# Attention over eight images in four layers: double banks for row scores, one product burst for two groups, small products moved into both bank rings

## The reference

```python
h = group_norm(x) * gamma + beta
q, k, v = w_qkv @ h + b_qkv          # per head: 16 x 1024
w = softmax((q.T @ k) / sqrt(16))    # per head: 1024 x 1024
out = x + w_proj @ (w @ v) + b_proj
```

## Time and profile before

| what | value |
|---|---|
| runs | 2506.1, 2512.8, 2544.4 us, median 2512.8 |
| profiled execution | 2514.5 us, span 2512.8 us |
| mean granted clock of TensorE | 0.948 of 2.4 GHz |
| PE busy | 2274.7 us (91%) |
| DVE busy | 1809.0 us (72%) |
| ACT busy | 1721.5 us (69%) |
| POOL busy | 401.3 us (16%) |

### The profile page before, as it was taken

How to read it: one execution, slowest core, us unless ns; L and a number is a source line. 1 busy time by engine, 2 the same in 40 slices (tenths; PEclk the granted TensorE clock), 3 DMA queues, 4 the chain that set the end, 5 groups by cost and what they waited for, 6 DMA issues and landing times. The chain is left out here.

```text
span 2512.8 us, 34220 instructions
## 1 busy us (share of the span) xinstructions
PE 2274.7 (91%) x11776; PEld 1093.3 (44%) x11776; DVE 1809.0 (72%) x3172; ACT 1721.5 (69%) x3107; POOL 401.3 (16%) x631
## 2 busy tenths in 40 slices
PE   2989898989999998989898989999897999999999
PEld 1333333333333333333333333333332788888887
DVE  1787878767784778687658767787871777777776
ACT  1377667657764676676547656766665888888887
POOL 3001010101101010101010101101001333333331
PEclk9999999989995899899869989999996999999999
DMA  7144251505333242516041505245110111111111
GB/s 142 14 58 62 40 88 28 87 25 79 53 50 57 46 61 42 72 34 95 18 60 41 87 16 87 41 61 70 37 35 27 53 62 61 52 45 55 61 48 45
DMA packets 63695, 137.64 MB, mean 55 GB/s; under 512 B 14880, under 2 KB 26272, under 8 KB 63392
## 3 DMA queue, kind: packets, MB, share of 16 engines
q1 hardware_dynamic: 60064, 133.90, 29.0%
q10 hardware_dynamic: 3456, 1.57, 0.4%
HBM read 57.31 MB, written 22.02 MB: 32 GB/s over the span
## 5 line engine op out<-in xcount | busy, mean ns | idle before, releaser
L463 DVE TENSOR_REDUCE h_half_nmax<-h_s_ps 128x1 f32<-128x512 f32 x2048 | 1287.8, 684 | 464.4 <-PE h_s_ps L705 451.5
L618 ACT ACTIVATE h_probs<-h_st_ps 128x512 f32<-128x512 f32 x2048 | 1086.4, 600 | 472.9 <-PE h_st_ps L842 468.5
L842 PE MATMUL h_st_ps<-h_qrep,h_krep 51*128 51x512 f32 x2048 | 699.7, 474 | 88.8 <-ACT h_probs L618 57.1
L705 PE MATMUL h_s_ps<-h_krep,h_qrep 48*128 48x512 f32 x2048 | 680.7, 495 | 106.9 <-DVE h_half_nmax L463 83.8
L705 PEld LDWEIGHTS h_s_ps<-h_krep,h_qrep 48*128 48x128 f32 x2048 | 281.4, 195 | 738.1 <-DVE h_half_nmax L463 633.1
L696 PE MATMUL h_pv<-h_probs,h_vT 128*32 128x512 f32 x4096 | 587.4, 648 | 0.0
L842 PEld LDWEIGHTS h_st_ps<-h_qrep,h_krep 51*128 51x128 f32 x2048 | 303.7, 195 | 321.7 <-ACT h_probs L618 202.6
L1364 PE MATMUL o_s<-o_k,o_q 128*128 128x512 f32 x768 | 224.5, 428 | 8.4 <-DVE o_q L1185 5.8
L1364 PE MATMUL o_pv<-o_pT,o_vT 128*128 128x512 f32 x768 | 208.1, 406 | 0.8 <-ACTq L1291 0.8
L1179 DVE TENSOR_TENSOR o_pT<-o_t,o_pT 128x512 fp32r<-128x512 f32 x256 | 164.5, 685 | 47.4 <-ACT o_pT L1316 44.9
L360 POOL TENSOR_SCALAR h_nparts<-h_nmax 128x16 bf16<-128x16 f32 x64 | 16.4, 256 | 1135.2 <-DVE h_nmax L471 1135.2
(11 more groups left out here) (108 smaller groups left out, 1255.5 us busy)
## 6 DMA issues: line engine op xcount, KB each, us to landing
h_krep<-h_kp SPq DMA_DIRECT2D x96, 256.0 KB, 9.3
h_qrep<-h_qp SPq DMA_DIRECT2D x192, 128.0 KB, 12.3
x_res<-out_dram SPq DMA_DIRECT2D x32, 512.0 KB, 3.4
num<-av SPq DMA_DIRECT2D x128, 64.0 KB
rrep<-rden_dram SPq DMA_DIRECT2D x16, 512.0 KB
out_dram<-o_y SPq DMA_DIRECT2D x16, 512.0 KB
h_x_in<-out_dram SPq DMA_DIRECT2D x15, 512.0 KB, 3.4
out_dram<-h_y SPq DMA_DIRECT2D x15, 512.0 KB, 2.7
```

The source lines that it names most:

```text
L463: reduce = nc.vector.tensor_reduce(half_nmax[:, c, column:column + 1], s_ps[bank(n + r)][:, :], AX.X, ALU.max, negate=True)
L618: nc.scalar.activation(probs[g % 2][:, j, :], st_ps[bank(n)][:, :], ACT.Exp, scale=1.0 / CH ** 0.5).then_inc(exp_done, 1)
L705: nc.tensor.matmul(s_ps[bank(n)][:, :], qrep[par][rows, th, m, tile * P:(tile + 1) * P], krep[par][rows, m, c * HALF:(c + 1) * HALF], star ...
L842: nc.tensor.matmul(st_ps[bank(n)][:, :], krep[par][rows, quad * 2 + m, st * P:(st + 1) * P], qrep[par][rows, th, quad * 2 + m, :], start=T ...
```

## The change

1. Row scores: two slots of two banks each. Both heads (`r` = 0, 1) of a half go into one slot, and VectorE reduces them with one instruction of 128x2x512.
2. Column scores: a ring of three banks, now over all uses in order. The bank `misc` is gone. What ScalarE reads (K0, K1, Q0, Q1, both transposes) takes a turn in this ring; what VectorE reads (average, values, output) takes a slot of the row ring. Values and output are each one job for both halves (`V`, `O` in place of V0, V1, O0, O1).
3. Products: for two groups at once, in even `k`. `probs` has four buffers for that.
4. Order of TensorE within a group: column scores 0, row scores 0 and 1, column scores 1, in even groups the products of the two groups before, then small products.
5. ScalarE no longer normalises or makes leading parts; GpSimd does both, over all 1024 columns at once. ScalarE issues the two DMAs of the rows of maxima right behind their copy, no longer behind the first exponential of the next group.

```diff
+    PROBS = 4
+    AVG, K0, K1, MAX1, Q0, Q1, V, MAX0, O = 0, 3, 4, 5, 6, 7, 8, 13, 14
+    FOR_ACT = (K0, K1, MAX1, Q0, Q1, MAX0)
+    COLUMN_BANKS = 3
+    ROW_SLOTS = 2
+    def places(last):
+        columns, rows = {}, {}
+        for s in range(4):
+            for k in range(GROUPS):
+                for j in range(QUAD):
+                    columns[s, k, j] = len(columns)
+                if (k in FOR_ACT if s % 2 == 0 else k in (MAX1, MAX0)) and not (last and s == 3 and k == MAX0):
+                    columns[s, k, "other"] = len(columns)
+                for c in range(2):
+                    if not (last and s == 3 and k + LEAD >= GROUPS):
+                        rows[s, k, c] = len(rows)
+                if s % 2 == 0 and k in (AVG, V, O):
+                    rows[s, k, "other"] = len(rows)
+        return columns, rows
...
-        s_ps = [psum(f"s_ps{i}", [P, HALF]) for i in range(BANKS)]
-        st_ps = [psum(f"st_ps{i}", [P, HALF]) for i in range(BANKS)]
+        s_ps = [psum(f"s_ps{i}", [P, 2, HALF]) for i in range(ROW_SLOTS)]
+        st_ps = [psum(f"st_ps{i}", [P, HALF]) for i in range(COLUMN_BANKS)]
         pv_ps = psum("pv", [P, HALF])
-        misc = psum("misc", [P, HALF])
...
-                pool.sem_inc(scale_ready, 1)
+                nc.gpsimd.tensor_scalar(h[:, :], x_in[:, :], co[:, 2:3], co[:, 3:4], ALU.mult, ALU.add).then_inc(h_ready, 1)
...
             def split(n, which):
                 pool.wait_ge(evacuated, n)
-                split_parts(nc.gpsimd, own, which)
+                own.done(nc.gpsimd.tensor_copy(parts[which][:, 0, :], full[which][:, :]))
+                own.done(nc.gpsimd.tensor_tensor(parts[which][:, 1, :], full[which][:, :], parts[which][:, 0, :].bitcast(F32),
+                                                 ALU.subtract))
...
+                reduce = nc.vector.tensor_reduce(half_nmax[:, c, th, :, pair % MP], s_ps[slot][:, :, :],
+                                                 AX.X, ALU.max, negate=True)
...
+            def max_rows(n, bank, step, th):
+
+                act.wait_ge(columns_ready, n)
+                own.done(nc.scalar.copy(mrow[th][:, :], st_ps[bank][:, :].bitcast(BF16)[0:MAX_PARTS * MH, 0:P]))
+                act.sem_inc(columns_done, 1)
                 par, quad = step // 2 % 2, step % 2
                 for r in range(2):
                     act.dma_start(qrep[par][r * ROWS + KS:r * ROWS + KM, th, quad * 2:(quad + 1) * 2, :].bitcast(F32),
...
                         column_scores(k, 0)
                         scores_ahead(k, 0)
+                        scores_ahead(k, 1)
                         column_scores(k, 1)
-                        if not (first and s == 0 and k == 0):
+                        if k % 2 == 0 and not (first and s == 0 and k == 0):
+                            products(k - 2)
                             products(k - 1)
-                        scores_ahead(k, 1)
-                        in_shared_bank(k)
+                        if (s, k, "other") in columns:
+                            for_act(k)
+                        if (s, k, "other") in rows:
+                            for_dve(k)
```

More of the change, by code:

```diff
@@ L457, in maximum, with output @@
-            def maximum(n, pair, c, offset=0):
-                th = pair // MP
[L460 to L472, removed]
+            def output(n, slot, nothing=False):
+                dve.wait_ge(rows_ready, n)
+                if nothing:
+                    own.done(nc.vector.tensor_copy(idle[:, :], s_ps[slot][:, 0, 0:2]))
+                else:
+                    own.done(nc.vector.scalar_tensor_tensor(
+                        out=y[:, :], in0=s_ps[slot][:, :, :].rearrange("p a t -> p (a t)"), scalar=wo[:, P:P + 1],
+                        in1=x_res[:, :], op0=ALU.add, op1=ALU.add))
+                dve.sem_inc(rows_done, 1)
+                dve.sem_inc(y_ready, 2)
@@ L476, in _ @@
                 statistics(part)
[L477 to L487, removed]
+            coefficients(1, 0)
+            own.done(values(2, 1, 0))
+            dve.sem_inc(rows_done, 1)
             dve.sem_inc(y_ready, 1)
-            dve.sem_inc(misc_for_dve, -3)
             for pair in range(LEAD):
                 for c in range(2):
-                    maximum(4 * (pair - LEAD) + 2 * c, pair, c, 4 * LEAD)
-            dve.sem_inc(scores_ready, -4 * LEAD)
+                    maximum(2 * pair + c + 3, c, pair, c)
+            dve.sem_inc(rows_ready, -(2 + 2 * LEAD))
             dve.wait_ge(g_in, 2)
@@ L651, in body @@
-                if not last:
-                    act.sem_inc(misc_for_act, -16)
+                        if (s, k, "other") in order:
+                            n = order[s, k, "other"]
+                            bank = n % COLUMN_BANKS
+                            if k == MAX1:
+                                max_rows(n + 1, bank, s, 1)
+                            elif k == MAX0:
+                                max_rows(n + 1, bank, s + 1, 0)
+                            else:
+                                evacuate(n + 1, bank, "k" if k in (K0, K1) else "q", int(k in (K1, Q1)))
@@ L668, in _, with project @@
         def _(pe):
-            def project(c, column, ready):
-                nc.tensor.matmul(misc[:, :], wg[:, column:column + P], h[:, c * HALF:(c + 1) * HALF],
-                                 start=True, stop=True).then_inc(ready, 1)
-            def project_values(c, of_next=False):
+            def project(bank, c, column):
+                nc.tensor.matmul(st_ps[bank][:, :], wg[:, column:column + P], h[:, c * HALF:(c + 1) * HALF],
+                                 start=True, stop=True).then_inc(columns_ready, 1)
@@ L681, in project_output @@
[L681 to L690 removed]
+                product.then_inc(rows_ready, 1)
@@ new lines, in project_output, with average, transpose_max @@
+            def project_output(slot):
+                for c in range(2):
+                    product = nc.tensor.matmul(s_ps[slot][:, c, :], wo[:, 0:P], attn[:, c * HALF:(c + 1) * HALF],
+                                               start=True, stop=True)
+                product.then_inc(rows_ready, 1)
+            def average(slot):
+                nc.tensor.matmul(s_ps[slot][:, 0, 0:2], gmat[:, :], st2[:, :], start=True, stop=True).then_inc(rows_ready, 1)
+            def transpose_max(bank, th):
+                nc.tensor.transpose(st_ps[bank][:, :].bitcast(BF16)[0:MAX_PARTS * MH, 0:P],
+                                    nparts[th][:, :, :, :].rearrange("p r a b -> p (r a b)"),
+                                    ident[:, :]).then_inc(columns_ready, 1)
@@ new lines, in for_dve @@
+                                combine_weights(nc, s_ps[slot][:, 0, :], wg)
+                            average(slot)
+                        elif k == V:
+                            project_values(slot, last and u == 1)
+                        elif first and u == 0:
+                            pe.sem_inc(attn_ready, 1)
+                            average(slot)
+                        else:
+                            pe.wait_ge(attn_ready, u + 1)
+                            project_output(slot)
```

403 lines of the change are left out of this document (146 added, 257 removed).

## The result

The change makes the kernel slower: 2734.9 us (median of 4 runs, 2725.9 to 2741.5) against 2515.8 (median of 4, 2506.1 to 2544.4), a ratio of 1.088 with an interval of 1.083 to 1.094. Forecast were 2616 us and a range up to 2710. The sign came out as forecast and so did the wait at the rows of maxima; the number of falls of the clock, and with it the size, did not. The profiled execution took 2738.4 us, of which 2736.7 are span.

The account below looks back on a forecast made before the run. TensorE and VectorE were taken to bind together, in series. From 2514.5 us, 16 x 0.7 for steps less 1.5 for the prologue gave 2524; clock terms +116 +38 -62 gave 2616 us, whole range 2410 to 2710.

Parts of the forecast that it names:

- The plain pair: Two groups sharing one burst of products: 5.70 us, or 2.85 a group instead of 2.94, keeping about 46 us.
- The rows of maxima: DMA issues ahead of the next even group's first exponential delay products: 1.8 us more, 7.5 a pair, 63 times.
- The steps at full clock: Sixteen-group steps of the many-head part: odd 50.2 us (+1.6), even 58.8 us (-0.9).
- the prologue: Work before the many-head steps: 24 double reductions of 1.14 for 48 of 0.60, -1.5 us.
- h on GpSimd: In even steps, 2.37 us to twice that, ready about 8 us in, before the key projection at 10.4; hidden.
- The clock: Largest term: falls to 1.2 GHz add 116 and 38 us, 62 returned; bounds -62 to +330-62.
- 63 x 0.8 x 2.3 = 116: Clock falls at four of five of the 63 maxima stretches, 2.3 us each: 116 us.
- The stretch behind values and outputs: Sparse 4.6 us of even steps, 41% work, with rare plain pairs: 16 falls of 2.4, 38 us.
- the 62 that the prediction gave back: Faster clock rise after five loop ends returns 54 us, start and tail 8.
- rival C: Clock falls in plain pairs too and stays low; half of 256 pairs low gives 370 more, near 2900 us; chance 0.07.
- A: Rival: clock stays up behind rows of maxima; 2524 us, or 2460 with loop ends returned, middle 2495; chance 0.28.
- B: Rival: early DMA issues don't delay products, maxima pair near 5.9 us; 2424 us, down to 2360; chance 0.20.

Follow-up runs that it names:

- e4: Changed kernel plus matmuls of a zero matrix, values unchanged, at places where TensorE waits; 2682.1 us.
- e1: Changed kernel with the two DMA issues of the rows of maxima put back behind the next group's first exponential; 2574.0 us.
- f3: Kernel of e3 with each double reduction cut into two of 512 columns, double slots kept; 2283.7 us.
- f4: Changed kernel with each double reduction cut into two of 512 columns; 2826.8 us.
- e3: Changed kernel with both late DMA issues and products of one group in every group; 2283.0 us.
- e2: Changed kernel with products of one group in every group, DMA issues still early; 2447.6 us.
- f1: Kernel before the change with only the DMA issues of the rows of maxima moved right behind their copy; 3033.3 us, ratio 1.208.
- f2: Kernel before the change with products of two groups at once and four exponential buffers, issues late; 2838.0 us, ratio 1.133.

## Why the prediction was right or wrong

**The plain pair: right.** Predicted 5.70 us at full clock, measured 3.72 + 1.93 = 5.65. The double burst was to take 1.86: 671.91 - 670.06 = 1.85. Double reductions were to cost 1.22 and 1.14; a row of two takes 2.36. VectorE's wait behind the burst, 1.1, is the 1.09 of the row.

**The rows of maxima: right, a little low.** Predicted were 1.8 us more for the pair, 7.5. At full clock the odd group takes 3.90 where a plain one takes 1.93, 1.97 more; 3.85 + 3.90 = 7.75. Two issues of 1.50 in all, then the exponential, then a bank: the chain of the prediction row for row.

**The steps at full clock, the prologue, GpSimd: small terms.** From the medians of each group at full clock (eight of the 32 that hardly ever have it are taken from e4, one from e1) a step would take 51.2 us odd and 59.9 us even, where 50.2 and 58.8 were forecast: about 16 x 2.1 = 34 us in all, 16 of them from the pairs at the rows of maxima. This is an estimate, since no whole step ran at full clock. h on GpSimd took 1.20 us (its row in the timeline at 735.02), not the 2.37 of the row taken for it; the whole wait of TensorE for it is 12.2 us in the page's groups, a single wait at 20 us in the prologue:

```profile
L623 PE MATMUL h_st_ps<-h_h,h_wg 128*128 128x512 f32 x136 | 80.7, 681 | 12.2 <-POOL h_h L348 12.2
```

The first group starts 85.9 us into the span instead of 90.3, so the prologue gave 4.4 where 1.5 was forecast; f3 and f4, with the reductions split again, still give 2.9 and 3.0. None of these decided anything.

**The clock: the step that failed.** The prediction's sum at an unchanged clock, 2524, stands on the terms above and is some 34 us low. Added to it were "63 x 0.8 x 2.3 = 116" and "The stretch behind values and outputs (4.6 us with eight pairs, 41%) and, rarely, a plain pair: 16 falls of 2.4, 38": 66 falls, 154 us. The record has 163. Sorted by place, 64 of them lie at the groups of the rows of maxima, somewhat more than the 50 counted on there. The other 99 lie elsewhere: 14 at the eleventh group of even steps, behind values, 5 at loop ends, and 80 in pairs that the prediction left at "rarely", such as the ninth and eleventh groups of odd steps, 16 times each in 16 steps. The 16 of the eleventh group come behind a statistics job that keeps TensorE waiting, so not all of the 80 are in quite plain pairs:

```profile
703.20 0.68 DVE L420 BATCH_NORM_STATS2 h_bst<-h_x_in 128x6 f32<-128x512 f32 x1
...
705.06 0.80 PE L661 MATMUL h_s_ps<-h_krep,h_qrep 48*128 48x512 f32 x2 [0.88 <-DVE h_half_nmax L474]
```

"Rarely, a plain pair" is the phrase that is wrong, by some 70 to 80 falls.

The price of a fall was over, not under: 2.3 was taken (its range was 1.7 to 2.5). The fifth group of odd steps takes 3.84 us at full clock and 5.44 with a low burst, 1.60 more; over the 46 groups that hold one short fall whole the median is 1.6 more than the same group at full clock. The total agrees roughly. The changed kernel's part is 229.7 us longer than before; less the 11 of unchanged clock, and with the 62 that the prediction gave back, 229.7 - 11 + 62 = 281, and 163 x 1.6 = 261 for the falls with the 34 from above are 295. How much of the 62 was given back no run shows apart. From e3 to e2 the two groups at a row of maxima go from 2.82 + 3.02 to 4.32 + 2.67, 63 x 1.15 = 72 us; the other 93 of the 165 go on 42 more falls, 2.2 each. With the right count and this price the forecast's own sum would have been 2524 + 261 - 62 = 2723: the count is what it lacked.

Why the count failed: the prediction had the number in hand. Under rival C it wrote that a plain pair has 50% of work between bursts, "about where it fell", against 52% at the place in the trace. It set that aside because "bursts should raise it". They do, and the next pairs bring it down again: a fall is short, and so there can be many. Rival C priced only a clock that stays low. The case between, many short falls in plain pairs, had no number of its own. The plain pair as a whole was booked as a gain of 46 us (0.18 x 256); taking the double burst out of it gave 287 us more (e2).

**The rivals.** A, the clock stays up: no. B, the issues do not delay the products: no, 3.90 against the 2.35 of e1, and the pair at 7.75 where under 6.4 would have decided for it. C: half true, as said; it falls in plain pairs and does not stay. Of the two rules of the Trainium skill, "TensorE: Matmul & The Clock Gate", that the prediction names, the trace sides with the section "A second HAM failure mode: psum-queue depth-cycling", by which short idles between groups of matmuls make the clock oscillate, and not with the table under "Why this matters for your kernels", which warns of long gaps between bursts: ahead of the fall at 681 us stand two plain pairs, with no TensorE gap over 1 us.

**What the sum left out.** The prediction put the gain of the new slots and banks at nothing apart from the bursts, since it priced the change as a whole: 2.85 us a group. With single bursts the same banks and the same order give 2.67 (e2, e3). The double burst takes most of that back (5.65 for two, 2.83 a group) and then costs clock.

## What to carry to other kernels

Where TensorE is not full, look first at how its work is spread, and reckon with a fall of the clock at every place that is as sparse as one where the trace shows a fall, however short the gaps. Collecting small matmuls into bursts makes the rest sparser; here it won a switch of about 0.1 us and lost 1.6 us at each fall. Issues of DMAs on an engine that is a link of the ring belong behind the instruction that others wait for, and one part of a change may pay well beneath two that cost: time them apart.

## What was not expected of the hardware

- Work that nobody needs made the kernel 53 us faster (e4): 639 more matmuls, clock 0.83 to 0.89 over the same 600 us.
- How long a fall lasts differs tenfold between kernels, and the cost goes with it. With single bursts in the old banks and order it is 253 / 6 = 42 us (before) and 1529 / 35 = 44 (f1); with double bursts there 891 / 144 = 6.2 (f2); with the new banks and order 737 / 163 = 4.5 with double bursts, and with single ones 335 / 48 = 7.0 (e2) and 92 / 6 = 15 (e3). So both the double burst and the new banks or order go with short falls; which property of them does it was not tried apart.
- In f1 a wait of 1.5 us at each row of maxima cost some 520 us; taking it out of the changed kernel (e1) gave back 161.
- What brings the clock down stays open in part: e4 filled the gaps after one guess, and of 163 falls 85 stayed.
